# A graph network kernel: GpSimd gathers eight rows, waits until they have landed, then gathers the next eight

## What is computed

```python
xi = x @ W_pre[:Fin]
xj = x @ W_pre[Fin:]
h = xi[dst] + xj[src] + b_pre
mean = segment_sum(h, dst) / degc
std = sqrt(relu(segment_sum(h * h, dst) / degc - mean * mean) + EPS_VAR)
mx = segment_max(h, dst)
mn = segment_min(h, dst)
agg = concatenate([mean, mx, mn, std])
out = concatenate([agg, agg * amp, agg * att])
out = concatenate([x, out]) @ W_post + b_post
return out @ W_lin + b_lin
```

## Time and profile before

| | us |
|---|---|
| median of 3 runs | 1782.25 |
| lowest and highest run | 1782.1, 1787.49 |
| span of the profiled execution | 2193.7 |
| the two scans in it (from the first row gather to the last row) | 647 to 1300, 1413 to 2071 |

### The profile page before, as it was taken

The page is one execution under the profiler, slowest core; times in us unless marked ns, Lnnn a source line. Parts: engine busy times, 40 slices in busy tenths (PEclk is TensorE's granted clock), DMA queues, the critical chain, the costliest instruction groups (busy, mean ns, idle before and its releaser), DMA issues.

```text
span 2193.7 us, 30278 instructions
## 1 busy us (share of the span) xinstructions
PE 1471.8 (67%) x11250; PEld 1048.3 (48%) x11250; DVE 1424.0 (65%) x2879; ACT 502.9 (23%) x1074; POOL 804.2 (37%) x831
## 2 busy tenths in 40 slices
PE   0277777667854777678677755457777777877553
PEld 0166777657842444445444543324444445544432
DVE  7899999691066665557556645666655566665447
ACT  3367677300031011111111110310111111111101
POOL 4400000032015455455554523155454555546230
PEclk9889898878986898889898887868888888888777
DMA  5223333234433455455555531344554555555320
GB/s 116 89 120 138 146 138 138 83 112 148 135 106 98 156 177 169 145 176 194 181 172 168 177 112 54 98 150 160 176 171 151 192 173 178 196 165 158 109 89 24
DMA packets 126239, 309.36 MB, mean 141 GB/s; under 512 B 21744, under 2 KB 73408, under 8 KB 125742
## 3 DMA queue, kind: packets, MB, share of 16 engines
q1 hardware_dynamic: 75216, 145.00, 18.7%
q10 hardware_dynamic: 23470, 105.20, 13.7%
q0 software_dynamic: 27440, 57.77, 9.8%
HBM read 167.18 MB, written 140.75 MB: 140 GB/s over the span
## 4 chain that ended last, share of the span: by engine, by line
DVE 36%; PE 31%; another core or an unknown queue 16%; issue 8%; DMA 4%; ACT 2%; POOL 1%; ACTq 1%; DVEq 0%; SPq 0%; POOLq 0%
PE ps L1139 14%; PE ps L1267 6%; DVE accs L2141 5%; DVE scanned L2170 4%; DVE accs L2123 4%; DVE scanned L1682 3%; DVE scanned L1679 3%; DVE scanned L1688 3%; PE ps L1279 2%; DMA A<-counts 2%; PE ps L1164 2%; PE ps L1367 2%; PE ps L1432 1%; DVE S L1655 1%
## 5 line engine op out<-in xcount | busy, mean ns | idle before, releaser
L1078 POOL DMA_INDIRECT scanned<-table,rest_idx x688 | 674.0, 980 | 796.7 <-DMA rest_history<-scanned 327.9
L1139 PE MATMUL ps<-big,A 125*128 125x128 bf16 (+1 forms) x7500 | 772.5, 259 | 104.6 <-issue 81.8
L1139 PEld LDWEIGHTS ps<-big,A 125*128 125x128 bf16 x7500 | 623.6, 104 | 249.6 <-issue 139.8
L1267 PE MATMUL ps<-S,big 126*128 126x500 bf16 (+1 forms) x1050 | 282.1, 413 | 264.1 <-DVE accs L2141 184.2
L2141 DVE TENSOR_TENSOR accs<-accs,ps 128x1000 f32<-128x1000 f32 (+1 forms) x154 | 166.8, 1083 | 402.4 <-remote 313.5
L2170 DVE SCALAR_TENSOR_TENSOR scanned<-scanned,rest_neg 128x256 f32<-128x256 f32 x688 | 331.8, 482 | 32.5 <-issue 6.0
L1267 PEld LDWEIGHTS ps<-S,big 126*128 126x128 bf16 x1050 | 102.6, 107 | 387.8 <-DVE accs L2141 205.7
L1164 PE MATMUL ps<-scanned 128*128 128x150 bf16 x1050 | 116.2, 253 | 76.1 <-DVE scanned L1688 75.1
L2123 DVE TENSOR_TENSOR accs<-accs,ps 128x1000 f32<-128x1000 f32 (+1 forms) x154 | 166.0, 1078 | 1.8 <-DVE MS L1796 1.1
L1096 POOL IOTA Y<- 128x784 int32 x1 | 0.8, 786 | 362.8 <-DVEq L1944 362.8
L1164 PEld LDWEIGHTS ps<-scanned 128*128 128x128 bf16 x1050 | 87.6, 132 | 92.5 <-issue 73.2
(11 more groups left out here) (384 smaller groups left out, 1409.8 us busy)
## 6 DMA issues: line engine op xcount, KB each, us to landing
rest_history<-scanned SPq DMA_DIRECT2D x172, 512.0 KB
A<-counts ACTq DMA_DIRECT2D x75, 800.0 KB
S<-picks SPq DMA_DIRECT2D x60, 640.0 KB
picks<-S ACTq DMA_DIRECT2D x25, 800.0 KB
counts<-A ACTq DMA_DIRECT2D x25, 800.0 KB
scanned<-table,rest_idx POOLq DMA_INDIRECT x688
table<-Y SPq DMA_DIRECT2D x10, 320.0 KB, 2.6
S<-picks SPq DMA_DIRECT2D x10, 160.0 KB
```

The source lines that it names most:

```text
L1078: nc.gpsimd.indirect_dma_start(out=lanes[:, r, s, 0:F], out_offset=None, in_=tables[1 + l], in_offset=bass.IndirectOffsetOnAxis(ap=rest_id ...
L1139: m = nc.tensor.matmul(acc[:, bank, 0:width], A[0:NB, slot, a, :], XS[0:NB, a, c, 0:width], start=a == 0 and c == 0, stop=a == NT - 1 and ...
L1267: m = nc.tensor.matmul(ps[:, bank + h, 0:len(blocks) * NB], XS[0:NB + 1, a, c, 0:F], pick[0:NB + 1, part % RING, 0:len(blocks), a % PART, ...
```

## The change

In `gather_rest`, behind the four gathers of each batch with an odd number, GpSimd waits until that batch has landed. The number of the batch within the scan is `k`, and `n` counts on over both scans. Line numbers behind it move by two.

```diff
                             out=lanes[:, r, s, 0:F], out_offset=None, in_=tables[1 + l],
                             in_offset=bass.IndirectOffsetOnAxis(ap=rest_idx[:, i:i + 1], axis=0))\
                             .then_inc(main.landed[r], 16)
+                    if k % 2:
+                        pool.wait_ge(main.landed[r], 16 * BATCH * ring_uses(r, n + 1))
                 finish_scan(main, l, [16 * ring_uses(r, (l + 1) * NBATCH) for r in range(LANES_RING)], rest_history,
                             P * REST, fixI[:, 1:2], restI)
```

## The result

The change made the kernel slower: median 1960.92 us (1955.55 to 1972.57, four runs) against 1782.17 us before (1780.73 to 1787.49), a ratio of 1.1005 with a 95% interval from 1.0973 to 1.1038. That is +179 us where +140 was forecast. (A ratio leaves out runs that are over 1.5% above the fastest of their kernel, so it can differ a little from the quotient of two medians, which are over all runs.)

A forecast was written before the change was run, and what follows sets the result against it. The prediction took GpSimd's row gathers as full when timed, with VectorE and TensorE close behind. Each scan gains 80 us of waits less 10 hidden: 2 x (80 - 10) = +140, 1782 + 140 = 1922 us, range 1815 to 2000.

The forecast's parts named there:

- These stalls belong to the profiled execution: In the scans: VectorE's unnamed waits and slow matmuls, about 405 us, explain the profile's extra 411 us, absent when timed.
- 448 us each: Both scans: 1308 us profiled less 411 of stalls leaves 897 us timed, 448 us for each scan.
- The count of slots: Check on scan length: 78 wide slots at 4.65 us and 13 light at about 3 make 402, plus the start.
- 344 x 1.28 = 440 us: GpSimd's row gathers in a scan: 344 rows at 0.98 us plus a 0.30 us gap, so GpSimd is nearly full.
- I take 1.9: Cost in us of each added GpSimd wait beyond the usual gap, with bounds 1.4 and 5.9; 42 waits make 80 a scan.
- The sign that was named: In the changed profile: gathers' idle time released by DMA scanned<-table, 50 to 84 times at 1.7 to 2.5 us each.
- I take off 10 us a scan: Part of the added waits hidden by GpSimd's head start, the six-batch ring and room between 440 and 448: 10 us a scan.
- The wait is hidden: Rival: GpSimd has room in the scans or the ring is nearly always full, so no change, 1782 to 1787 us; chance 0.14.
- The bulk loads: Rival: GpSimd's pauses speed the first picks' loads at scan start, 4 us gained, 1778 us; most of faster's 0.06.
- Slow landing: Rival: transfers crowd through the whole scan, a wait costs 3 us or more, 2024 us; beyond 2000 some 0.04.
- TensorE at its lower level: A slower TensorE clock in the scans is no second loss: it would have to take TensorE beyond GpSimd's 520 us.
- The loads of instructions: Possible source of the stalls: 56 loads on one queue, 16 KB each, 0.92 MB, about as many as the stalls.

The follow-up runs named there:

- The fixed delay: Kernel before, with six small GpSimd instructions, each waited for, at the 43 places of a scan where the change waits: 1938.64 us against 1782.3 on a first-kind chip.
- the 1794 us kernel: The change, but at the same 43 places GpSimd waits for the pair's first batch, not its second: 1794.27 us against 1782.3 for the kernel before, first-kind chip.

## Why the prediction was right, and where it was wrong

**The sign and the mechanism: right.** The prediction held that GpSimd was full when timed although the first profile showed it half idle, so that a wait for the last gather's landing comes on top. The fixed delay shows that time added to GpSimd there is time added to the kernel, and the wait for the first of the pair shows that the same wait is free if its batch has landed.

**"These stalls belong to the profiled execution": wrong.** That step laid 411 us to the profiler. Chips of the second kind took 2112 to 2174 us in 32 runs of the kernel before, and on a first-kind chip a profiled execution is as short as the others. The first profile looks like those of the second kind in its nameless waits and its waits for stores, and in its span within 20 us of the longest of these runs; the times beside it are those of the first. Its conclusion, that the timed runs had no stalls, was true of these runs, but by luck of where they ran. With this step falls the forecast of a longer profiled execution, 2250 to 2275 us: the spans of the changed kernel are 1962.5 and, on a second-kind chip, 2058.7 us, both below the 2193.7. And the record of the lift is not missing, as the prediction had it; its semaphore comes late.

**"448 us each": too low.** On a first-kind chip the profile of the changed kernel has 623 + 96 + 109 = 828 us outside the scans, which leaves 1782 - 828 - 2 = 952, or 476 us a scan; the 1794 us kernel has 478 and 491. The 411 us were not all in the scans: 2194 - 653 - 657 = 884 us lay outside in the first profile, 56 more than 828. The count of slots that seemed to agree, 402 us, was still further off.

**"344 x 1.28 = 440 us": right.** A gather takes 0.997 us on average in the changed kernel and 1.007 in the 1794 us one, and the usual gap is 0.30: 446 to 450.

**"I take 1.9": mis-sized.** The sign that was named did show, a new releaser 67 times and `negate` waiting for its batch 165 times instead of 15, but at 3.08 us and not 1.7 to 2.5. A wait costs 2.7 us over the usual gap, between the bounds of 1.4 and 5.9 and above the 1.31 to 2.30 on which the choice leaned. The landings seen by ScalarE in the earlier trace rows include two of 1.6 and 2.6, and one of 6.24 that I set aside as the crowd at the start of a scan. In the changed kernel the median from issue to landing is 3.7 us, the longest 7.2, so the crowding is not only at the start: in a first-kind chip's scan the DMA engines are 58 to 69% busy, where the page before had 51%. The fit that the Trainium skill gives ("DMA: Bandwidth & Descriptors", "Anatomy of one DMA — SWDGE (gpsimd) path"), 2.15 us for 64 KB, lies below even the shortest landing of 2.4 us; the measurement decides.

**"I take off 10 us a scan": too little.** 42 x 2.7 = 113 us were added to GpSimd in a scan and 89 showed, so 24 were hidden. About 10 us of waits for stores and for VectorE were there to be filled, as much as was taken off. The end of the scan was put at nothing, and it is the other part: in the 1794 us kernel VectorE's last row comes 17 us after the last gather has been issued (478 against 461 us from the first gather), in the changed one 5 us (565 against 560), so 12 us are hidden there. So two terms were off, by +34 and -14 us a scan, and the net by 20 a scan, the 39 us between 1922 and 1961.

**The rivals.** *The wait is hidden* did happen, where its condition held: on second-kind chips. There it even turned into a gain. *The bulk loads* were right to be small: TensorE's wait for the first picks is 28.7 us with the change and was 29.4. *Slow landing* was the direction in which the size was off: it had 3 us for a wait and 10 hidden in all, 2024 us, where 2.7 us and 48 hidden were measured. *TensorE at its lower level* was rightly no second loss: with the change its granted clock in the scans is 0.91 where the 1794 us kernel has 0.96 and 0.94, and it is busy for 450 and 445 us instead of 421 and 423, well below the 565.

**What stays open** is what the stalls are. On second-kind chips TensorE waits for nothing that the trace shows, GpSimd's pauses for the last gather take most of it away, and pauses for the first of a pair, or for every fourth batch, don't. In the scans that fits a cause that needs many gathers queued, together with something of the chip. But it can't be the whole, as TensorE stalls on second-kind chips before the first row gather too. Its count matmuls between 396 and 585 us, in the kernel before on a second-kind chip and in the change on a first-kind one:

```profile
L1139 PE MATMUL ps<-big,A 125*128 125x128 bf16 x1844 | 123.5, 229 | 34.1 <-DMA A<-counts 14.1 <-issue 12.1 <-ACT A L762 4.7
```

```profile
L1141 PE MATMUL ps<-big,A 125*128 125x128 bf16 x1950 | 116.4, 223 | 23.0 <-DMA A<-counts 17.6 <-ACT A L762 4.7 <-ACT MS L749 0.6
```

The 12.1 us under "issue" are in every second-kind profile (12 to 16 us), with or without the change, and in none of the first kind. In the scans the same row has 45 to 66 us in the kernel before, 57 with the wait for the first of a pair, 75 with a wait for every fourth batch, 8 with the change and 0 with a wait for every batch. The loads of instructions, which the prediction named, are unlikely to be it: 56 in the profiles from either kind of chip, 62.6 us together in both of the profiles just quoted, and the stalls begin at any distance behind a load. No run here shows the cause, and the gain on a second-kind chip rests on one execution of the change.

## What to carry to other kernels

A profile belongs to the execution that it was taken of: if its span is far from the timed runs, don't explain the difference by the profiler before the two have been seen on one chip, and don't read which engine has room from it. An engine that is busy half the time by the page can be full once what stalls the others is gone; add up its own instructions and the usual gaps and hold the sum against the length of the stage. A wait for one's own last transfer costs its whole landing, here 3 us; the same wait for the one before it, issued 5 us earlier, cost a fifteenth of that.

## What was not expected of the hardware

- One program, 1782 us on some chips and 2143 us on others, each within its own narrow range (1779 to 1787, 2112 to 2174). Outside the scans the second kind is 50 to 60 us behind, in the scans of the kernel before about 130 to 160 us each.
- On a second-kind chip a pause of GpSimd for its last gather made the kernel 3.8% quicker (one execution), on one of the first kind 10% slower.
- A row gather of 64 KB took 3.7 us from issue to landing (median; 2.4 to 7.2), while GpSimd was busy for 0.94 us of it.
- On a second-kind chip a matmul's semaphore came up to 14 us after the end that the profile gives the matmul, and the wait for it was then listed without a name.
